# A gated cross-attention stack on one core: the last feed-forward layer as one-expert tiles instead of all maps per row

## The reference, cut to what matters

```python
def _L1_ffn_ref(x, tile_sigs, W, b):
    scores = jnp.einsum('bsd,td->bst', x, jnp.sign(tile_sigs))
    idx = jnp.argmax(scores, axis=-1)
    all_out = jnp.einsum('bsd,tde->bste', x, W) + b[None, None]
    out = jnp.take_along_axis(all_out, idx[:, :, None, None], axis=2)
    return out[:, :, 0, :]
x = x + tanh(g_xattn[0]) * _L0_xattn_ref(_layernorm(x), ctx_1024, ...)
x = x + tanh(g_ffn[0]) * _L0_ffn_ref(_layernorm(x), ...)
x = x + tanh(g_xattn[1]) * _L1_xattn_ref(_layernorm(x), ctx_1024, ...)
x = x + tanh(g_ffn[1]) * _L1_ffn_ref(_layernorm(x), L1_ffn_tile_sigs, L1_ffn_W, L1_ffn_b)
```

## Time and profile before

| what | value |
|---|---|
| median of 3 runs | 575.72 us (572.73 to 576.63) |
| the profiled execution | span of 572.2 us from first to last instruction; the runs' times lie 0.5 to 4.4 us above it |
| PE busy | 518.1 us, 91% of the span |
| POOL, DVE, ACT busy | 366.0, 397.8, 341.6 us |
| first expert layer's tiles | loads issued from 139.0 to 208.0 us |
| second attention | signatures from 255.6 to 554.8 us |

### The profile page before, as it was taken

The page is one execution under the profiler, slowest core; times in us unless marked ns, Lnnn a source line. Parts: engine busy times, 40 slices in busy tenths (PEclk is TensorE's granted clock), DMA queues, the critical chain, the costliest instruction groups (busy, mean ns, idle before and its releaser), DMA issues.

```text
span 572.2 us, 14118 instructions
## 1 busy us (share of the span) xinstructions
PE 518.1 (91%) x3611; PEld 335.8 (59%) x3611; DVE 397.8 (70%) x1174; ACT 341.6 (60%) x997; POOL 366.0 (64%) x781
## 2 busy tenths in 40 slices
PE   6878886699999996899999999999999999999952
PEld 5767775456566655565656565665656565656520
DVE  3868887375334433578888888888888888888631
ACT  3667775322455552787676767677676767676510
POOL 4665888774255554346777777777777786777442
PEclk9978997599999999999999999999999999999965
DMA  9934620131122221000000000000000000000000
GB/s 229 154 72 132 174 60 16 37 85 46 43 75 79 76 62 38 10 6 15 11 13 18 9 18 9 18 9 18 9 18 9 18 9 18 9 9 5 10 10 5
DMA packets 32280, 23.79 MB, mean 42 GB/s; under 512 B 7897, under 2 KB 29793, under 8 KB 32210
## 3 DMA queue, kind: packets, MB, share of 16 engines
q1 hardware_dynamic: 29250, 17.86, 12.8%
q0 software_dynamic: 2272, 4.67, 2.5%
q10 hardware_dynamic: 720, 0.82, 0.6%
HBM read 16.57 MB, written 8.39 MB: 44 GB/s over the span
## 4 chain that ended last, share of the span: by engine, by line
PE 69%; POOL 5%; DVE 3%; DMA 3%; issue 3%; ACT 3%; POOLq 0%; SPq 0%; DVEq 0%; ACTq 0%
PE bank L1318 12%; PE bank L1266 11%; PE bank L1279 8%; PE bank L1257 8%; PE bank L1002 4%; PE bank L1253 3%; PE bank L1290 2%; PE bank L1327 2%; PE bank L1018 2%; DMA xs<-sorted_x 2%; PE bank L956 2%; PE bank L957 2%; PE bank L967 2%; PE bank L1306 1%; PE bank L1244 1%
## 5 line engine op out<-in xcount | busy, mean ns | idle before, releaser
L1367 ACT ACTIVATE PRT<-bank 77x512 f32<-77x512 f32 x128 | 74.7, 584 | 17.7 <-PE bank L1266 15.7
L1266 PE MATMUL bank<-cst,wgu 128*77 128x128 f32 x512 | 81.0, 281 | 1.0 <-ACT wgu L1359 1.0
L1318 PE MATMUL bank<-w,xn3T 128*128 128x512 f32 x128 | 75.0, 668 | 2.5 <-DVE XN L1514 2.0
L1266 PEld LDWEIGHTS bank<-cst,wgu 128*77 128x77 f32 x512 | 59.5, 150 | 15.5 <-issue 13.9
L1359 ACT ACTIVATE wgu<-wgu,low 128x77 f32<-128x77 f32 x256 | 67.4, 346 | 1.3 <-DVE low L1460 0.2
L946 POOL DMA_INDIRECT routed<-ys,to x39 | 37.4, 959 | 45.0 <-DVE ys L1149 34.1
L1446 DVE TENSOR_TENSOR wgu<-bank,biasQ 128x616 f32<-128x616 f32 x64 | 51.1, 799 | 11.5 <-PE bank L1257 9.9
L1514 DVE TENSOR_TENSOR XN<-bank,OH 128x512 f32<-128x512 f32 x64 | 44.3, 692 | 16.3 <-PE bank L1318 10.8
L1279 PE MATMUL bank<-PRT,VP 77*32 77x128 f32 x1024 | 54.5, 285 | 0.5 <-ACT PRT L1367 0.5
L1453 DVE TENSOR_REDUCE top<-wgu 128x8 f32<-128x616 f32 x64 | 50.5, 789 | 1.1
L1257 PE MATMUL bank<-KB,QT 32*128 32x308 f32 x256 | 50.7, 472 | 0.0
(11 more groups left out here) (231 smaller groups left out, 1268.1 us busy)
## 6 DMA issues: line engine op xcount, KB each, us to landing
xs<-sorted_x SPq DMA_DIRECT2D x39, 64.5 KB, 1.8
wgu<-in_wgu SPq DMA_DIRECT2D x4, 512.0 KB
y<-routed SPq DMA_DIRECT2D x32, 64.0 KB, 1.8
out<-res SPq DMA_DIRECT2D x32, 64.0 KB, 1.6
ctxT<-in_ctxT SPq DMA_DIRECT2D x16, 77.0 KB, 2.9
mask<-in_mask SPq DMA_DIRECT2D x16, 77.0 KB, 3.4
wdn<-in_wdn SPq DMA_DIRECT2D x2, 512.0 KB
X<-in_x SPq DMA_DIRECT2D x1, 768.0 KB, 5.7
```

The costliest lines, as they stand in the source:

```text
L1266: last = nc.tensor.transpose(bP[c % 2][0:SK, j * 128:j * 128 + 128], SC[u][:, c * HG + j, :], ident)
L1318: nc.tensor.matmul(bF[:, :], xn3T[u][:, :], w2[:, k * HT:(k + 1) * HT, :], start=True, stop=True).then_inc(s["f"], 1)
L1367: nc.scalar.activation(PT[c % 2][:, :], bP[c % 2][0:SK, :], ACT.Copy if c * HG < HH else ACT.Exp).then_inc(s["pTs"], 1)
```

## The change

The last layer leaves the second attention and becomes a stage of its own behind it, built as the expert layer is. In `attend_1` the choice, the maps, the picks, the sums and the stores go; a batch ends with its 8 scores copied (`copied`). The residual x3 is kept for all batches in `XN`, in rows of 132 elements (x3, the place in the output, a zero, and the norm's scale and shift). At the ends of groups of batches (`RANKED`) DVE and PE rank the rows by expert, and POOL scatters the 132-element rows of each batch to DRAM, one batch per turn at first and two later. Behind the attention SP overwrites the ends of the 8 regions, DVE works out the table of tiles, and 39 tiles follow: load, norm on ACT, transpose, one map and one bias row on PE, sum on DVE, a scatter to the output that leaves rows outside alone. All loops of `attend_1` are written out (`turns`).

```diff
+WX = D + 4
+RANKED = [0, 8, 16, 24, 28, 30, 32]
...
-def pipeline(eng, n, stages, ways=2, begin=None):
...
+def turns(n, stages):
+    written_out(n, [((lambda item, stage=stage: stage(item, item % 2)), lag) for stage, lag in stages])
...
-        XN = sb("XN", [128, B, D + 1])
+        XN = sb("XN", [128, B, WX])
-        b2 = sb("b2", [T, D])
+        b2 = sb("b2", [1, T, D])
...
+        *[(m["sorted_y"][E * REGION + 128 * k:E * REGION + 128 * k + 128], a["outside"]) for k in range(DUMPS)],
...
         def norm3_T(b, u):
             pe.wait_ge(s["xn3"], b + 1)
-            wait(pe, s["x3b"], b)
+            wait(pe, s["zTs"], b)
+            wait(pe, n["s"]["lgs"], b)
+            wait(pe, n["s"]["wh"], 2 * n["before"](b) - 1)
...
-        pipeline(pe, B, [
-            (signature, 5), (weigh(0), 3), (probs_T(2), 3), (weigh(1), 3), (probs_T(3), 3), (choice_T, 5),
-            (project, 4), (weigh(2), 3), (maps(0), 5), (scores(1), 2), (weigh(3), 3), (maps(1), 5),
+        turns(B, [
+            (signature, 5), (weigh(0), 3), (probs_T(2), 3), (weigh(1), 3), (probs_T(3), 3),
+            (project, 4), (weigh(2), 3), (n["ranks"](pe), 5), (scores(1), 2), (weigh(3), 3),
             (shared("queries"), 0), (queries, 1), (shared("T0"), 0), (probs_T(0), 2), (heads_T, 3),
-            (picked_bias, 5), (shared("sc01"), 0), (scores(0), 1), (norm3_T, 4), (probs_T(1), 2),
+            (shared("sc01"), 0), (scores(0), 1), (norm3_T, 4), (probs_T(1), 2),
             (mixed_T, 3), (shared("norm_T"), 0), (norm_T, 0)])
...
-            nc.vector.tensor_tensor(x3[u][:, :], bB[:, 0:128], x2b[u][:, :], ALU.add).then_inc(s["x3"], 1)
+            nc.vector.tensor_tensor(XN[:, b, 0:D], bB[:, 0:128], x2b[u][:, :], ALU.add).then_inc(s["x3"], 1)
...
-        pipeline(dve, B, [
-            (choose, 5), (shared("bias0"), 0), (bias(0), 2), (shared("max0"), 0), (maxima(0), 2),
-            (lower(0), 2), (residual, 4), (pick(0), 5), (shared("bias2"), 0), (bias(1), 2),
-            (shared("stats2"), 0), (stats2, 0), (pick(1), 5), (shared("max1"), 0), (maxima(1), 2),
-            (add_bias, 5), (shared("mix"), 0), (mix, 3), (shared("sub1"), 0), (subtract(1), 2)])
+        turns(B, [
+            (n["copied"](dve), 5), (n["route"](dve), 5), (shared("bias0"), 0), (bias(0), 2), (shared("max0"), 0),
+            (maxima(0), 2), (lower(0), 2), (n["slots"](dve), 5), (residual, 4), (shared("bias2"), 0), (bias(1), 2),
+            (shared("stats2"), 0), (stats2, 0), (shared("max1"), 0), (maxima(1), 2),
+            (shared("mix"), 0), (mix, 3), (shared("sub1"), 0), (subtract(1), 2)])
...
-        pipeline(pool, B, [
-            (inv2, 1), (values, 2), (total, 6), (keys, 1), (with_bias, 2), (stream, 0), (inv3, 4)])
+        turns(B, [
+            (inv2, 1), (values, 2), (keys, 1), (with_bias, 2), (stream, 0), (inv3, 4), (n["scatters"](pool, s["nb3"]), 6)])
...
+def feed_forward_1(nc, sb, sem, sems, bank, out, m, f):
...
+        at, item = {}, 0
+        for b in range(B):
+            item = max(item, groups[group_of(b)][1] - 1)
+            at.setdefault(item, []).append(b)
+            if len(at[item]) == (1 if item < RANKED[3] - 1 else 2):
+                item += 1
+        def stage(item, u):
+            for b in at.get(item, []):
+                pool.wait_ge(s["slot"], group_of(b) + 1)
+                pool.wait_ge(normed, b + 1)
+                nc.gpsimd.indirect_dma_start(sorted_y, bass.IndirectOffsetOnAxis(ap=slot[:, b:b + 1], axis=0),
+                                             XN[:, b, :], None).then_inc(s_scat, 16)
...
+    def sp_program(sp):
+        sp.wait_ge(s_fill, 2)
+        for k in range(T):
+            row = sp.value_load(fill_rows[0:1, k:k + 1], min_val=0, max_val=E * REGION - 128)
+            sp.dma_start(sorted_y[bass.ds(row, 128), :], m["outside"]).then_inc(s_filled, 16)
+        sp.wait_ge(s_filled, 16 * (E + T))
+        sp.wait_ge(s_table, 2)
+        sp.wait_ge(s_scat, 16 * (B + B))
+        for t in range(NTILE):
+            row = sp.value_load(tile_rows[0:1, t:t + 1], min_val=0, max_val=E * REGION + (DUMPS - 1) * 128)
+            sp.wait_ge(e["ys"], done + t - WAYS + 1)
+            sp.dma_start(xs[way(t)][:, :], sorted_y[bass.ds(row, 128), :]).then_inc(l_x[way(t)], 16)
...
+    def pool_program(pool):
+        for t in range(NTILE):
+            pool.wait_ge(e["ys"], done + t + 1)
+            nc.gpsimd.indirect_dma_start(out.rearrange("b s d -> (b s) d"), bass.IndirectOffsetOnAxis(ap=to[:, t:t + 1], axis=0),
+                                         ys[way(t)][:, :], None, bounds_check=B * S - 1,
+                                         oob_is_err=False).then_inc(st_y[way(t)], 16)
...
+        written_out(NTILE, [(maps, 2), (rows_T, 0)])
...
+        def norm(t):
+            act.wait_ge(l_x[way(t)], 16 * (turn(t) + 1))
+            act.wait_ge(e["xT"], done + t - 1)
+            x = xs[way(t)]
+            nc.scalar.activation(xn[t % 2][:, :], x[:, 0:D], ACT.Identity, bias=x[:, D + 3:D + 4],
+                                 scale=x[:, D + 2:D + 3]).then_inc(s["xn"], 1)
...
+        written_out(NTILE, [(rows_T, 1), (norm, 0)])
...
+        def result(t):
+            dve.wait_ge(e["y"], done + t + 1)
+            wait(dve, st_y[way(t)], 16 * turn(t))
+            x = xs[way(t)]
+            nc.vector.scalar_tensor_tensor(out=ys[way(t)][:, :], in0=bY[t % 2][:, 0:D], scalar=x[:, D + 1:D + 2], in1=x[:, 0:D],
+                                           op0=ALU.add, op1=ALU.add).then_inc(e["ys"], 1)
+        written_out(NTILE, [(result, 2), (place_of, 0)])
```

More of the change, by code:

```diff
@@ L90, with segment_at @@
 C_ROW = C_TILE + NTILE
-C_END = C_ROW + B
+C_SEGS = C_ROW + B
+SIZES = sorted({b - a for a, b in zip(RANKED, RANKED[1:])})
+C_END = C_SEGS + sum(E * (q + 1) for q in SIZES)
+def segment_at(q):
+    first = C_SEGS + sum(E * (k + 1) for k in SIZES if k < q)
+    return slice(first, first + E * (q + 1))
 def constants():
@@ L1216, in attend_1 @@
     s = sems("d", "set clear x2 x2b st2 mv2 v2 nb2 xn2 xT xTs q qs kb vp sc sb mx su lo ex pT pTs pv os oT "
[L1217 to L1218 removed]
+                  "rd ao aT aTs y x3 st3 mv3 v3 nb3 xn3 zT zTs")
     l_y = [sem(f"d_y{u}") for u in two]
@@ L1228, in stage @@
             def stage(b, u):
-                for n in range(*(PE_SHARED.get((place, b), (0, 0)) if isinstance(b, int) else (0, 0))):
+                for n in range(*PE_SHARED.get((place, b), (0, 0))):
                     j, part = piece(n)
@@ L1338, in stage @@
             def stage(b, u):
-                for n in range(*(ACT_SHARED.get((place, b), (0, 0)) if isinstance(b, int) else (0, 0))):
+                for n in range(*ACT_SHARED.get((place, b), (0, 0))):
                     j, k = divmod(n, HC)
@@ L1393, in norm3_T @@
             act.wait_ge(s["zT"], b + 1)
-            wait(act, s["f"], 2 * (b - 1))
+            wait(act, n["s"]["lg"], b - 1)
             nc.scalar.activation(xn3T[u][:, :], bF[:, 0:128], ACT.Copy).then_inc(s["zTs"], 1)
-        def choice_T(b, u):
-            act.wait_ge(s["hT"], b + 1)
-            wait(act, s["fb"], b - 1)
-            nc.scalar.activation(OHT[u][:, :], bF[0:T, 0:128], ACT.Copy).then_inc(s["hTs"], 1)
-        pipeline(act, B, [
+        turns(B, [
             (shared("pe0"), 0), (probs_T(0), 2), (shared("norm2"), 0), (norm2, 0), (norm3_T, 4),
-            (probs_T(1), 2), (mixed_T, 3), (shared("xTs"), 0), (norm_T, 0), (probs_T(2), 2), (choice_T, 4),
+            (probs_T(1), 2), (mixed_T, 3), (shared("xTs"), 0), (norm_T, 0), (probs_T(2), 2),
             (probs_T(3), 2), (exps(0), 1), (heads, 2), (shared("qs"), 0), (queries, 0), (norm3, 3)])
@@ L1421, in stage @@
             def stage(b, u):
-                for n in range(*(DVE_SHARED.get((place, b), (0, 0)) if isinstance(b, int) else (0, 0))):
+                for n in range(*DVE_SHARED.get((place, b), (0, 0))):
                     j, part = piece(n)
@@ L1550, in stream @@
             wait(pool, s["x2b"], b - 1)
-            if isinstance(b, int) and b == LAST_STATIC:
+            if b == LAST_STATIC:
                 pool.wait_ge(h["add"], EARLY + LATER)
-            landed(pool, l_y, b, u)
-            one = lambda t: t[u][:, :].rearrange("p (o d) -> p o d", o=1)
-            nc.gpsimd.tensor_tensor(one(x2), X[:, bass.ds(b, 1), :], one(y), ALU.add).then_inc(s["x2"], 1)
+            pool.wait_ge(l_y[u], 16 * (b // 2) + 16)
+            nc.gpsimd.tensor_tensor(x2[u][:, :], X[:, b, :], y[u][:, :], ALU.add).then_inc(s["x2"], 1)
         def with_bias(b, u):
```

317 lines of the change are left out of this document (207 added, 110 removed).

## The result

| | before | after | predicted |
|---|---|---|---|
| median of the runs | 576.17 us (572.73 to 577.95, 4 runs) | 653.08 us (652.69 to 653.69, 4 runs) | 606 us (575 to 630) |
| profiled span | 572.2 us | 650.9 us | 602.6 us |
| first signature | 255.6 | 257.4 | 255.6 |
| 31 gaps of the second attention | 299.2 | 301.9 | 262.6 |
| tail behind the last signature | 17.4 | 91.6 | 84.4 |

The ratio is 1.134, interval 1.130 to 1.138. The change is slower, as forecast, but by 77 us instead of 30, outside the range. Of the 48.3 us by which the span exceeds the forecast, 39.3 lie in the attention: taking the maps out of PE gave nothing back at all. Of each kernel, executions more than 1.5% above its fastest count in no ratio or interval; medians and ranges take in all.

A forecast was written before the change was run, and what follows sets the result against it. It took PE, always busy at 2.4 GHz, to bound the second attention. Start 255.6, 31 gaps 262.6 and tail 84.4 gave a span of 602.6 us, 30.4 above 572.2, so 606.1 us; range 575 to 630.

The forecast's parts named there:

- What bounds the kernel: Second attention: PE busy all the time at 2.4 GHz, one batch 9.75 us, 7.24 without maps and picked bias.
- the turns without scatters: Second attention, first 8 gaps: the loop of the exponentials sets 7.74 us each, 61.9 us in all.
- the predicted wait at T0: First transposes of the probabilities, second attention: without the maps PE waits 0.5 us there in each batch.
- The loop over POOL: Second attention: x3, inv3, scatter of 1.41 us, inv2, norm2, norm_T, signature and back to x3, 8.50 us.
- the step that counted 16 x 8.50 and 3 x 9.76 at the full clock: Second attention: 16 gaps with one scatter, 136.0 us, and three with two, 29.3 us.
- The terms of the 31 gaps: Second attention: 61.9, 136.0, 29.3, 25 for the last four gaps and 10 for groups, sum given as 262.6 us.
- Group ends: Second attention, four times: DVE's ranking operations ahead of bias0 and the residual add 2.5 us each (bounds 1.5 and 3).
- The tail: Behind the last signature: fills, first load at 19.2 us, 39 tiles at 1.4 us, end at 84.4 us against 17.4.
- The loop of three tiles through four buffers: Tail: load t waits for result t-4; one loop of 3.7 to 4.6 us carries three tiles, 1.2 to 1.5 each.
- Rival (1): Second attention: scatters hidden, exponentials' loop governs, gaps 240 us, time 583.5 us; chance 0.20.
- Rival (2): Second attention runs at PE's own 7.24 us a batch, gaps 220.5 us, time 564 us, faster; chance 0.10.
- Rival (3): Tail tiles run at the first expert layer's 1.82 us, 16 us more, time 622 us; chance 0.15.

The follow-up runs named there:

- e2: Changed kernel plus two useless 128x256 matmuls on PE ahead of norm_T from row 13 on; 633.16 us (1.100).
- e1: Changed kernel with POOL's scatter moved behind keys, where POOL waits for the residual, instead of between inv3 and inv2; 604.62 us (1.047).
- e11: e1 with rows ranked in groups of four rather than eight up to row 24, three more group ends; 609.13 us (596 to 620).
- e8: e5 with eight tile buffers in place of four; 593.68 us (1.028).
- e5: e1 with every second fill of the tail issued by ACT instead of SP; 598.05 us (1.040).
- e9: e8 plus useless PE matmuls in the tail: 20 of 128x256 behind the last ranks, one of 128x256 per tile; 586.32 us (1.017).
- e10: e8 without the matmul that adds the picked expert's bias; 583.97 us (1.014).
- e7: e8 plus useless PE matmuls in the tail: 20 of 128x256 behind the last ranks, one of 128x128 per tile; 595.66 us.
- e6: e5 plus useless PE matmuls in the tail: 20 of 128x256 behind the last ranks, one of 128x256 per tile; 611.88 us.
- e3: Changed kernel plus useless PE matmuls in the tail: 30 of 128x256 behind the last ranks, one of 128x128 per tile; 665.64 us.

## Why the prediction was wrong, step by step

**What bounds the kernel, and the turns without scatters: right.** The first seven gaps are 7.73 us, with the predicted wait at T0, though it is 0.22 us (at 285.44) and not 0.5: PE is busy for 7.5 us of a batch and not for 7.24.

**The loop over POOL: right in mechanism, 0.76 us short.** Three of its terms were too small. From the end of inv3 to the next instruction the scatter holds POOL for 1.65 us (337.96 to 339.61), not 1.41. Norm2 to residual is 3.25 us (341.30 to 344.55), not 3.16. And inv2 takes 1.65 us, not 1.23: its first operation lasts 0.60 instead of 0.19 us. That one ends at 340.21, with DVE's subtract L1426 (340.17). In the 19 turns with a scatter up to 520 us it lasts 0.52 to 0.62 us wherever it overlaps the subtract (11 times) and 0.20 to 0.21 wherever it doesn't (8 times), as here:

```profile
370.08 0.20 POOL L1493 TENSOR_TENSOR v2e<-mv,eps 128x1 f32<-128x1 f32 x1
```

The scatter had pushed inv2 under the subtract. The prediction took from the Trainium skill (SBUF — State Buffer, section Who interferes with whom) only the rule on the two-port mode, and found no such operation here; the same section says that a VectorE instruction with two inputs in SBUF contends with a GpSimd instruction that reads SBUF, and the subtract is one. The trace agrees with that sentence: 0.3 to 0.4 us in each of the 11 turns. Twelve of the 39.3 us come from the loop's 0.76 us (16 x 0.76).

**What failed: the step that counted 16 x 8.50 and 3 x 9.76 at the full clock.** The prediction weighed the clock for the tail alone. Where it forecast a PE that rests 15% of each turn (8.50 - 7.24 us), it did not ask what the granted clock does then, though the earlier trace rows showed 0.50 where PE rests. The rest lets the clock fall; while it is low PE's instructions take longer (four transposes 1.14 in place of 0.66 us); the turn takes 10.0 to 12.9 us. e2 prices it at 23 us or more, and e1 shows that with the scatter elsewhere both the longer loop and most of the low clock go, 54 us together. The terms of the 31 gaps also add up to 262.2 us and not to the 262.6 written, which changes nothing here. The Trainium skill describes such a pattern for PE waiting on DMA in every tile, with the clock lost again each time (TensorE: Matmul & The Clock Gate, section HAM oscillation — how this bites in real kernels); the runs here show it with a wait for another engine, in about half of the turns (0.62 in the window from 360, 1.00 in that from 340).

**Group ends: 1.5 us where the clock holds (e11), 2.5 forecast**, the lower bound that was given. The one at 311.5 took 11.2 us in the changed kernel, with a clock of 0.66 in the window from 315.

**The tail: right in its parts, the pace mis-sized.** Up to the first load 17.2 for 19.2 us. The pace of 1.66 for 1.40 us costs 10 us more. The loop of three tiles through four buffers was taken for the bound, and its three matmuls of 0.52 us at half the clock were not added up as PE's own work on a tile: 1.56 us by the forecast's own figures, above the 1.4 it took, and 1.555 as measured. Two bounds lie close together: eight buffers alone give 5 us less tail (e8: 594.8 - 512.3 = 82.5, e5: 594.5 - 507.0 = 87.5, e1: 92.1), and only with PE relieved, by clock or by work, does it come to 75.1 (e9) and 73.8 us (e10).

**The rivals.** Rival (1), the scatter hidden, is what e1 does: 247.7 us of gaps for the 240 that it gave. Rival (2) needed gaps under 7.49 us, and none was seen in a regular turn, e1's included. Rival (3), the slow pace of the tail, came halfway (1.66 of 1.82).

No version of this study beats the kernel before. The best complete one, e9, stands at 1.017 (e10 leaves out the bias, and e7's shortest execution, 577.71 us, still lies above the 575.96 measured beside it). Even a start of 257.4, 31 gaps of 7.74 us and a tail of 74 would make a span of 571 us where 572.2 stood: the exposed last layer would cost as much as the maps did. What was not tried: another form for the picked bias, or ranking in DVE's idle time.

## What to carry to other kernels

Removing work from the engine that bounds a stage pays only down to the next loop, and if the same change puts a slow instruction into that loop, the loop is what the time follows: look for a place in the in-order queue where the engine waits anyway (here 2.83 us on POOL, worth 48 us). When a forecast makes TensorE rest in every turn, price the turn at the low clock too. A stage moved behind everything else is paid in full, so add up each engine's work per item at the clock that an idle TensorE is granted.

## What the hardware showed beyond expectation

- In turns of 9.26 us with a rest of about 1.2 us the granted clock fell to 1.2 GHz for some microseconds, in about half of the turns; it came back soon after, and fell again in a later turn. In the tail it fell with a rest of 0.95 us in e7 and held through one of 1.21 us in e6. What decides is open.
- PE's row can be full at either level: 59.46 of 60.00 us at 0.50 in e3, 40.00 of 40.00 at 0.50 in e8, 40.00 of 40.00 at 1.00 in e9. In e3 the clock was back at 1.00 during the matmuls without use behind the ranks (560 to 570), and at 0.50 again among the tiles.
- In every tail POOL's output scatters stop once, for 1.7 to 3.5 us, behind the tenth. In the changed kernel the tenth starts at 598.09 and the next at 602.20, though DVE had its input ready at 598.89. The cause is open.
